# A two-layer recurrence on one core: early inputs in two loads, the first steps rearranged, layer 1's last step in fp32

## What is computed

```python
def step(carry, xw_t):                    # layer 0; xW = x @ Wx + b
    prev_h, prev_c = carry
    a = xw_t + prev_h @ Wh                # 4 gates of 128
    i = sigmoid(a[:, :H]); f = sigmoid(a[:, H:2*H]); o = sigmoid(a[:, 2*H:3*H])
    g = tanh(a[:, 3*H:])
    next_c = f * prev_c + i * g
    next_h = o * tanh(next_c)
...
def step(h, xt):                          # layer 1, on x + layer 0's output
    m = concatenate([xt, h]) @ weight + bias
    c = tanh(m[:, units:]); g = sigmoid(m[:, :units] + 1.0)
    h_new = g * h + (1.0 - g) * c
...
x = x + layer0(x, cond); x = x + layer1(x, cond)
```

## Time and profile before

| | |
|---|---|
| median of 3 runs | 227.15 us (226.89 to 231.1) |
| profiled execution, its own time | 227.22 us |
| its span in the trace | 225.4 us |
| busy: TensorE, VectorE, ScalarE, GpSimd | 98%, 89%, 59%, 1% |
| granted TensorE clock, mean | 0.995 |
| first DMA issues | 0.72 us (ScalarE's queue), 0.73 us (SyncE's queue) |

### The profile page before, as it was taken

The page is one execution under the profiler, slowest core; times in us unless marked ns, Lnnn a source line. Parts: engine busy times, 40 slices in busy tenths (PEclk is TensorE's granted clock), DMA queues, the critical chain, the costliest instruction groups (busy, mean ns, idle before and its releaser), DMA issues.

```text
span 225.4 us, 12289 instructions
## 1 busy us (share of the span) xinstructions
PE 220.5 (98%) x4842; PEld 206.9 (92%) x4842; DVE 200.1 (89%) x1365; ACT 133.6 (59%) x903; POOL 2.5 (1%) x10
## 2 busy tenths in 40 slices
PE   8999999999999999999999999999999999999994
PEld 6899999999999999999999999999999999999882
DVE  5889988989989998998998988998998999899895
ACT  3665565565566566665656666666656656666551
POOL 2200000000000000000000000000000000000000
PEclk9999999999999999999999999999999999999998
DMA  6000001001111001010010000101011000100000
GB/s 191 25 17 23 17 26 48 17 25 31 32 29 31 13 26 49 16 29 26 23 41 26 21 21 28 49 15 28 26 33 34 26 15 26 28 16 15 16 4 25
DMA packets 11876, 6.69 MB, mean 30 GB/s; under 512 B 1318, under 2 KB 11692, under 8 KB 11820
## 3 DMA queue, kind: packets, MB, share of 16 engines
q1 hardware_dynamic: 11664, 5.72, 8.9%
q10 hardware_dynamic: 156, 0.20, 0.3%
HBM read 3.82 MB, written 2.10 MB: 26 GB/s over the span
## 4 chain that ended last, share of the span: by engine, by line
PE 87%; DVE 10%; ACT 1%; issue 1%
PE a L291 16%; PE gate_f L264 13%; PE a L248 8%; PE a L282 8%; PE gate_f L231 5%; PE gate_i L231 5%; PE gate_o L231 4%; PE gate_g L231 4%; PE gate_i L270 4%; PE gate_o L270 4%; PE gate_g L270 3%; PE a L284 2%; PE gate_g L274 2%; PE a L328 1%; DVE cell_bank L615 1%; PE a L253 1%
## 5 line engine op out<-in xcount | busy, mean ns | idle before, releaser
L264 PE MATMUL gate_f<-hT,w_f 128*128 128x32 f32 x254 | 48.0, 271 | 0.3
L264 PEld LDWEIGHTS gate_f<-hT,w_f 128*128 128x128 f32 x254 | 37.8, 188 | 8.2 <-DVE hT L622 7.6
L513 ACT ACTIVATE gate_f<-gate_f 128x32 f32<-128x32 f32 x127 | 23.1, 182 | 37.5 <-PE gate_f L264 37.4
L533 ACT ACTIVATE act_bank<-cell_bank 128x32 f32<-128x32 f32 x128 | 23.3, 182 | 33.4 <-DVE cell_bank L615 33.4
L615 DVE TENSOR_TENSOR_SCAN cell_bank<-act_bank,scan_add 128x64 f32<-128x64 f32 x128 | 38.2, 298 | 0.4 <-ACT act_bank L513 0.3
L539 ACT ACTIVATE acts<-a 128x64 f32<-128x64 f32 x128 | 28.6, 223 | 14.4 <-PE a L291 1.9
L282 PE MATMUL a<-h_high,w1x_scaled 128*128 128x32 f16 x256 | 35.3, 176 | 0.3 <-DVE w1x_fp L605 0.3
L282 PE MATMUL a<-h_high,w1x_rest 128*128 128x32 f16 x256 | 35.4, 176 | 0.0
L282 PE MATMUL a<-h_high,w1x_third 128*128 128x32 f16 x256 | 35.4, 176 | 0.0
L284 PE MATMUL a<-h_low,w1x_fp 128*128 128x32 f16 x256 | 35.3, 176 | 0.0
L622 DVE TENSOR_TENSOR hT<-out_gate,act_bank 128x32 f32<-128x32 f32 x128 | 23.9, 187 | 10.5 <-ACT act_bank L533 10.3
(11 more groups left out here) (117 smaller groups left out, 1042.1 us busy)
## 6 DMA issues: line engine op xcount, KB each, us to landing
early<-in_x_dram SPq DMA_DIRECT2D x45, 64.0 KB, 1.9
out_dram<-outT SPq DMA_DIRECT2D x32, 64.0 KB, 1.6
early<-in_early_dram SPq DMA_DIRECT2D x1, 272.0 KB, 2.8
w_raw<-in_L_cond_weight_dram SPq DMA_DIRECT2D x2, 128.0 KB, 3.4
wh_raw<-in_L_cond_Wh_dram ACTq DMA_DIRECT2D x1, 192.0 KB, 2.9
w_f<-in_forget_dram SPq DMA_DIRECT2D x1, 128.0 KB, 3.4
bias_rows<-in_biases_dram ACTq DMA_DIRECT2D x1, 3.0 KB
```

The costliest lines, as they stand in the source:

```text
L264: nc.tensor.matmul(gate_step(GATE_F, j), w_f[:, P:2 * P], hT[:, (j - 1) % RING, :], start=False, stop=True, skip_group_check=True).then_in ...
L513: return nc.scalar.activation(out, gate_step(q, j), func)
```

## The change

Six things are changed; the steps from the second body to the seventh keep their code.

- **Loads.** `early` comes in two loads on SyncE's queue: first i's projection weights, cond and x (144 KB, semaphore `x_in[0]`), then those of g and o (128 KB, `wx_in`). The biases are loaded by GpSimd's queue, ahead of the identity matrix, and ScalarE's queue begins with `wh_raw`. `WARM` is 11.
- **Splitting the weights.** ScalarE scales `wh_raw` in two pieces (256 and 128 columns), VectorE splits both before the first scan. GpSimd forms `w1x_rest` in two halves, each when its half is scaled, and `w1x_third` behind `w1x_fp16`. VectorE makes `w1x_fp16` ahead of step 1's forget product and `w1h_rest` and `w1h_third` one step later each.
- **First steps on TensorE.** Projections and bias matmuls change places; layer 1's state part is in fp32 in two steps (j of 2 and 3) instead of one (`layer1_whole`).
- **Semaphore counts** of `layer1_rest` and `layer1_low` go down by one, since one step less makes them.
- **Last half body.** The warm-ups at k = 1 and 3 stand at the step's end and write to the other bank; at k = 5, 6 and 7 there are three, one and four.
- **Layer 1's last step.** `layer1_last` sums the candidate in its own bank (the free one of gate g), with its own projection and bias, and the state's part of both halves is two fp32 matmuls in place of twelve bf16 ones. ScalarE takes two tanh of 128 x 32. VectorE (`last_result`) makes the output as x1 + u/4 + c/2 + (z/2)(u/2 - c), all of which but two operations can precede the gate z. The last store is in two parts, of three steps (48 KB) and one (16 KB).

```diff
-WARM = 13
+WARM = 11
...
+            pool.dma_start(bias_rows[:, :], b).then_inc(b_in, 16)
             nc.gpsimd.memset(ident[:, :], 0.0).then_inc(ident_zero, 1)
...
-            sp.dma_start(early[:, 0:N + 3 * P + HS * N], early_in).then_inc(x_in[0], 16)
+            sp.dma_start(early[:, 2 * P:3 * P + N + HS * N], early_in[:, 2 * P:]).then_inc(x_in[0], 16)
+            sp.dma_start(early[:, 0:2 * P], early_in[:, 0:2 * P]).then_inc(wx_in, 16)
             load_x(1, 1)
...
             warm(WARM)
             pe.wait_ge(x_in[0], 16)
             project0(GATE_I, 0, 3)
+            pe.wait_ge(wx_in, 16)
             project0(GATE_O, 0, HS)
...
-                    if ends and k in (1, 3):
-                        warm(2, False)
                     if in_parts:
                         layer1_rest(r, l)
...
+                    if ends and k in (1, 3):
+                        warm(2, a1[0][:, 2 * P:4 * P], False)
                     if ends and k > 4:
-                        warm(2 if k == 6 else 4)
+                        warm({5: 3, 6: 1, 7: 4}[k])
...
-            act.dma_start(bias_rows[:, :], b).then_inc(b_in, 16)
             act.dma_start(wh_raw[:, :], wh).then_inc(wh_in, 16)
...
+            def layer1_last(j):
+
+                pe.wait_ge(scan_in_ready, 2 * T - 1)
+                nc.tensor.matmul(last_candidate, w1_raw[:, 0, P:2 * P], xT[:, j * N:(j + 1) * N],
+                                 start=True, stop=False, skip_group_check=True)
+                nc.tensor.matmul(last_candidate, bias_lhs[:, :], pick[:, NG + 1:NG + 2].to_broadcast([P, N]),
+                                 start=False, stop=False, skip_group_check=True)
+                pe.wait_ge(acts1_ready, T - 1)
+                pe.wait_ge(low_ready, T)
+                sums = ((1, last_candidate), (0, a1_step(j)[:, 0:N]))
+                for q, to in sums:
+                    for weights in parts_of(w1x_scaled, w1x_rest, w1x_third, q):
+                        nc.tensor.matmul(to, weights, h_high[:, j % PARTS, :],
+                                         start=False, stop=False, skip_group_check=True)
+                    nc.tensor.matmul(to, w1x_fp16[:, q * P:(q + 1) * P], h_low[:, j % PARTS, :],
+                                     start=False, stop=False, skip_group_check=True)
+                pe.wait_ge(u_ready, T)
+                for q, to in sums:
+                    nc.tensor.matmul(to, w1h_scaled[:, q * P:(q + 1) * P], u_of(j - 1),
+                                     start=False, stop=True, skip_group_check=True).then_inc(a1_summed, 1)
```

More of the change, by code:

```diff
@@ L201, in _, with body @@
                 load_x(SLOTS + ahead, SLOTS + ahead)
-            def body(b, load, load_ahead):
+            def body(b, load, load_ahead, last=False):
                 for c in range(SLOTS):
@@ L214, in body @@
                         load_x(h + SLOTS, c)
-                    store(h, c)
+                    if last and c == SLOTS - 1:
+                        o = (HS - 1) * N
+                        sp.wait_ge(out_ready, HALVES)
+                        sp.dma_start(out_h[h][:, 0:o], outT[:, c, 0:o]).then_inc(last_half, 16)
+                        sp.wait_ge(out_ready, HALVES + 1)
+                        sp.dma_start(out_h[h][:, o:], outT[:, c, o:]).then_inc(out_free[c], 16)
+                    else:
+                        store(h, c)
             body(0, True, True)
@@ L229, in project0 @@
                 k = (first - BEGIN[q]) % GS
[L230 removed]
+                weights = w_f[:, 0:P] if q == GATE_F else wx_s[q]
                 return nc.tensor.matmul(gate_banks[q][:, k * N:(k + steps) * N], weights,
@@ L400, in body @@
                         project0(GATE_F, a, a_steps)
-                    if k == 1:
+                    opens = first and m == 0
+                    if k == 1 and not opens:
                         if not ends:
@@ L498, in _ @@
             act.wait_ge(wh_in, 16)
-            nc.scalar.activation(wh_scaled[:, :], wh_raw[:, :], ACT.Copy,
-                                 scale=1.0 / LIFT).then_inc(wh_scaled_ready, 1)
+            for columns in (slice(0, 2 * P), slice(2 * P, 3 * P)):
+                nc.scalar.activation(wh_scaled[:, columns], wh_raw[:, columns], ACT.Copy,
+                                     scale=1.0 / LIFT).then_inc(wh_scaled_ready, 1)
             def scale_input(q):
@@ L682, in body @@
                     l0, l1 = [(j - back) % BODY for back in (1, 2)]
-                    layer1_runs, in_parts = not (first and j < 2), not (first and j < 3)
+                    layer1_runs, in_parts = not (first and j < 2), not (first and j < 4)
                     if not (first and j == 0):
@@ L752 @@
         "x": xt,
-        "early": _np.concatenate([_np.asarray(inputs["cond_1024"]).T, wx[:, d:], xt[:, :HS * n]], axis=1),
+        "early": _np.concatenate([wx[:, q * d:(q + 1) * d] for q in EARLY_GATES]
+                                 + [_np.asarray(inputs["cond_1024"]).T, xt[:, :HS * n]], axis=1),
         "L0_cond_Wh": wh[:, d:],
```

171 lines of the change are left out of this document (99 added, 72 removed).

## The result

| | before | changed |
|---|---|---|
| median | 227.02 us (226.61 to 231.1, 4 executions) | 232.05 us (231.69 to 232.12, 4 executions) |
| profiled execution, its own time | 227.22 us | 231.69 us |
| its span | 225.4 us | 229.8 us |

The ratio is 1.0209, 95% interval 1.0179 to 1.0238. The kernel has become slower by 4.7 us (5.0 by the medians) where I had forecast 1.6 us less; that the loss is above 2%, for which I had given 0.01, isn't clear, since the interval has 2% inside it. The executions of the kernel before fall into two groups, near 227 and near 231, and the ratio compares all four of the changed kernel, near 232, with those of before that lie near 227; what the two groups are is the subject of the experiments.

A forecast was written before the change was run, and what follows sets the result against it. The prediction took 128 recurrent steps of 1.67 us (214 of 225.4) as the bound. Savings of 0.25 + 0.35 + 0.08 + 0.30 + 0.59 = 1.57 us from 227.15 gave 225.6, range 225.0 to 226.7.

The forecast's parts named there:

- The step that failed: TensorE's start: eleven warm-ups end at 3.25, gate_i runs in the time TensorE waited; 0.25 us saved.
- rival (c): TensorE's clock rises one step later with two fewer warm-ups: 1.0 us, so 226.6; chance 0.05.
- Rival (a): GpSimd's biases land at 4.1 or a little over, first scan 0.3 to 0.5 late: 226.2; chance 0.18.
- My own sign of being wrong: VectorE's start: the prediction is wrong if, among other signs, the biases come behind 4.
- The term of +0.25 for the start: The start: 0.25 us saved on TensorE's side, between 0.1 and 0.45; VectorE's side doesn't bind before it.
- The two loads: Early inputs at the start: the first 144 KB take 2.2 us and land at about 3.0.
- my worst case: TensorE's start: both parts of the early inputs held back by the weights until about 4.2; 0.1 us saved.
- Steps 1 and 2: First two steps: h_low and VectorE's work behind the scan get shorter; 0.35 and 0.08 us saved.
- Steps 3 to 9: fp32 state sums, projections and biases change places one for one: nothing, with 0.15 us either way.
- The last eight steps: Moved warm-up matmuls shorten four long steps: sum 0.34, taken as 0.30 us saved.
- The end: Behind the last hT: store issued 0.49 us sooner and smaller; 0.59 us saved, between 0.3 and 0.75.
- my 0.1: Last store of 16 KB instead of 64: 0.1 us saved, between nothing and 0.2.

The follow-up runs named there:

- e1: The changed kernel with 13 warm-up matmuls instead of 11: 226.95 us median, ratio to the kernel before 0.999.
- e3: The kernel before with 11 warm-up matmuls instead of 13: 231.75, 230.77, 231.77 and 227.27 us.
- e4: The changed kernel with 15 warm-ups and the biases loaded by ScalarE's queue ahead of the state's weights: 226.41 us, ratio 0.9974.
- e2: The changed kernel with 15 warm-up matmuls instead of 11: 227.1 us, ratio to the kernel before 0.9997.
- e8: e4 with 11 warm-ups first and the other four between the first and the second projection: 226.82 us median, ratio 0.9994.
- e11: The changed kernel with its 11 warm-ups, the biases loaded by ScalarE's queue: 226.16, 226.31, 231.19 and 231.61 us.
- e6: e4 with the early inputs in one load of 272 KB again: 226.47 us, ratio 0.9982.
- e9: The kernel before with 15 warm-up matmuls instead of 13: 227.18 us, ratio 0.9986.
- e7: e4 with the warm-ups of the last half body at their old places: 227.0 us, ratio 1.0021.
- e5: e4 with the last store in one piece of 64 KB again: 226.26 us, ratio 0.9967.
- e12: The kernel before with 15 warm-ups and three unused semaphores: 227.65 us in one execution.
- e10: The kernel before with 15 warm-ups and the changed kernel's end, nothing of its start: 226.54 us, ratio 0.9965.

## Why the prediction was wrong, step by step

**The step that failed** is the one at the start where "the warm-up at 2.93 / 13 = 0.225 us each ends, with eleven, at 3.25" and gate_i begins earlier. I costed the two warm-ups at nothing but their own time, that is, I took it that the clock comes as before. They are what brings it: one number, WARM, moves either kernel by 4 to 5 us (e1, e3). That it is the clock is read from TensorE's durations; that it is WARM is shown. The mechanism was there as rival (c), with 0.05 and 1.0 us. Its price was wrong by a factor of four to five, because I let the clock come "one step later" when the traces have it before 6 us or near 19, and in between TensorE, busy all the time by the timeline, makes five steps of 2.3 to 3.0 us its own. Its chance was wrong as well: the times of before held an execution at 231.1 beside 226.89 and 227.15, which I took for a disturbance. It was the same thing in the kernel before, at 13 of 57, to go by the counts: none of those executions has a profile, but e3's have the same times, and with 15 warm-ups they are gone.

**Rival (a), the biases.** I let the first bias operation come at 3.3, with 4.1 as the far end; it came at 4.30. GpSimd's issue began at 1.22, 0.5 later than the 0.7 that I reckoned from, and lasted 0.76, and the 3 KB landed 3.1 us after it; on ScalarE's queue they are read 1.6 after theirs. The identity matrix came late too, but VectorE had 0.64 us to wait for the biases behind it. My own sign of being wrong, biases behind 4, came true. The mechanism was right: four operations (1.05) and the splits (1.1) behind e1's first bias operation at 4.36 give a scan at 6.51, and it starts at 6.53. With an early clock (e1) the first hT is at 7.10, 0.58 behind the kernel before, and with the biases on ScalarE's queue (e4) the median is 0.7 lower than e2's. The term of +0.25 for the start should have been -0.58. This is the second term that failed, and WARM hides it in the changed kernel.

**The two loads.** My interpolation, 2.2 us for 144 KB, is exactly what e4 measured, and 3.0 is what the changed kernel had; the first part being held back by the weights too I had only in my worst case. And even with the inputs at 3.06 nothing was earned: the first projection behind 15 warm-ups starts its weight load at 3.6 to 3.9, and with fewer the clock is at risk (e8, e11). One load is as good (e6).

**Steps 1 and 2** gave 0.33 (e1: 3.53 us against 3.86), predicted 0.43. Against e9, the old code with the early clock and 3.68 us for the two steps, only 0.15 is left; of what e9 is shorter than before, 0.17 is its shorter h_low. And in the changed code h_low's stretch did not go as I had said. GpSimd is not done when h_low starts, here in e1 (first two lines), and h_low takes 0.31; in e9 (last two) it takes 0.20:

```profile
6.85 0.83 POOL L186 TENSOR_TENSOR w1x_rest<-w1x_scaled 128x128 f32<-128x128 f32 x2 [2.39 <-ACT w1x_scaled L541]
7.42 0.31 DVE L676 SCALAR_TENSOR_TENSOR h_low<-hT,h_high 128x32 f16<-128x32 f32 x1
...
6.15 0.84 POOL L177 TENSOR_TENSOR w1x_rest<-w1x_scaled 128x256 f32<-128x256 f32 x1 [1.93 <-DVE wh_third L601]
6.84 0.20 DVE L629 SCALAR_TENSOR_TENSOR h_low<-hT,h_high 128x32 f16<-128x32 f32 x1
```

So of the 0.18 that h_low was long, only 0.06 went. The less of it lies beside `w1x_rest`, the shorter it is: 0.37 with 0.32 us in common, 0.31 with 0.26, 0.20 with 0.15. That goes with my reading of the cause, but GpSimd's spans are rough, and no run takes its work away. What w1h_rest behind the scan gave was not separated by an experiment either.

**Steps 3 to 9** I set to nothing within 0.15; from the third to the eleventh hT e1 takes 13.77 us and before 13.73.

**The last eight steps** gave 0.33, predicted 0.30; e7 undoes it. This term was right in mechanism and in size.

**The end** up to the last store: 0.39 to 0.40, predicted 0.49. The gate's tanh came at 226.76, 0.92 behind the state's operation (225.84), where I had 0.89. Behind the store my 0.1 was of the wrong sign: the changed kernel ends 2.3 us after the issue, before 1.97. This took back most of the end's gain in that profile. It isn't the short rows of the last store: its 16 KB landed 1.4 us after their issue, where a store of 64 KB takes 1.6 at the median. The split of the store (e5), GpSimd's load (e4) and the semaphore count (e12) are excluded, by one profile each, and e10 puts it with the new end; what of that does it stays open.

With the clock equal, then, the change is worth nothing that these runs can tell from zero: e1 against before 0.999 (0.9951 to 1.003). Its end earns 0.6 us by the medians (e10 against e9), its bias load and its queue order lose as much (e4 against e2).

**Which version is best.** e5 (the changed kernel, 15 warm-ups, biases on ScalarE's queue, one last store) has 226.26 us, ratio 0.9967 (0.9939 to 0.9996) to before, so some 0.3% faster, 5.8 us under the changed kernel's median, and none of its ten executions was above 227.03. e10 is its equal.

## What to carry to other kernels

A warm-up is not filler until the data arrive: here its length decided whether TensorE had its full pace in the first steps (late in 9 of 12 executions with 11, in 14 of 61 with 13, in none of 55 with 15), so it can't be shortened to the landing of a load. Look at every single time of a kernel before costing it: one value of three that is 2% off may be a second course of the same program, and a small edit can make it the only one. Compare profiles only when the pace of their starts is the same, and read that from the length of an instruction. A small load that gates an in-order engine did better here on ScalarE's queue ahead of the large one than on GpSimd's (0.7 us by the medians), and the load that was needed first landed sooner too.

## What the hardware did that I had not expected

- In the changed kernel TensorE stayed at the lower pace (0.50 to 0.55 us for a pair of fp32 weight loads) up to 18.96 us although the timeline has it busy without a gap from 3.81 on. The Trainium skill, "TensorE: Matmul & The Clock Gate", Part 1, has the clock rise after sustained activity and says that the moment varies from run to run. That it varies is what these runs show too: with 15 warm-ups, the higher pace is there at 3.58 in the profile of e5 and only after 5.44 in that of e12. Sustained work alone, as the timeline counts it, did not bring it in the changed kernel before 19 us; what else decides it, no run here shows.
- A load of 3 KB by GpSimd's queue landed 3.1 us after its issue and blocked GpSimd for 0.76 us; by ScalarE's queue it was read 1.6 to 1.8 us after the issue. The Trainium skill, "DMA: Bandwidth & Descriptors", Specifications, gives the two kinds of queue first-byte latencies 0.4 us apart; measured here to the use of the data, GpSimd's later turn included (its issue starts 0.5 us after ScalarE's), the difference is 1.8 to 2.0.
- 144 KB took 2.2 us to land where another queue's 192 KB were issued 0.6 us later (e4), and 3.0 where they were issued at the same time (the changed kernel, e2).
- `h_low`, the same VectorE operation on 128 x 32, took 0.37 us in the kernel before and 0.31 in e1 beside GpSimd's `w1x_rest`, and 0.19 in the next step of both.
